# Router step of the second half moved ahead of the first half's final layer norm, and five weight tensors stored partition-major

## The reference

```python
x = x + _layernorm(_L0_attn_ref(_layernorm(x), ...))
x = x + _layernorm(_L0_ffn_ref(_layernorm(x), ...))

# attention: conv of width 3 (4096 -> 3072), q/k/v projections 1024 -> 1024,
# causal attention inside blocks of 128 tokens, 16 heads of 64,
# output projection wo (1024 -> 1024), then proj_w (1024 -> 4096)

# ffn
logits = einsum('bsh,he->bse', hidden_states, gate_w)        # 8 experts
routing_weights, _ = top_k(logits, 2)
h = relu(hidden_states @ up_w) ** 2                          # 4096 -> 8192
shared_out = h @ down_w                                      # 8192 -> 4096
x_latent = hidden_states @ fc1_w                             # 4096 -> 2048
expert_out = x_latent @ expert_w                             # 2048 -> 2048
moe_out = expert_out * sum(routing_weights)                  # one number per token
routed_out = moe_out @ fc2_w                                 # 2048 -> 4096
return _layernorm(shared_out + routed_out)
```

## Time and profile before

| | |
|---|---|
| median of 3 runs | 4912.88 us (4912.10 to 4917.04) |
| the profiled execution | 4912.69 us |
| its span on the slowest core (core 4) | 4911.6 us |
| spans of the 8 cores | 4874.0 to 4911.6 us |
| TensorE busy | 3857.2 us, 79% of the span |
| VectorE, ScalarE, GpSimd busy | 761.7, 488.3, 273.3 us |
| granted TensorE clock, mean of a core | 0.906 to 0.910 of full speed |

### The profile page before, as it was taken

The page is one execution under the profiler, slowest core; times in us unless marked ns, Lnnn a source line. Parts: engine busy times, 40 slices in busy tenths (PEclk is TensorE's granted clock), DMA queues, the critical chain, the costliest instruction groups (busy, mean ns, idle before and its releaser), DMA issues.

```text
span 4911.6 us, 43172 instructions; the slowest of 8 cores (4874.0 to 4911.6 us)
## 1 busy us (share of the span) xinstructions
PE 3857.2 (79%) x18033; PEld 1726.2 (35%) x18033; DVE 761.7 (16%) x1126; ACT 488.3 (10%) x797; POOL 273.3 (6%) x369
## 2 busy tenths in 40 slices
PE   1699999999548711889998999970779998999960
PEld 1244444444223201334443444430334443444420
DVE  4300000000460144110000000027110000000027
ACT  2100000002213411001111000002001111000001
POOL 0000000000000022000000000000000000000000
PEclk9999999999769855899999999995899999999985
DMA  5144444446002243668887776763578887677743
GB/s 160 35 75 75 76 75 75 75 77 103 0 1 44 62 161 150 122 115 153 152 152 139 135 144 130 143 127 123 112 123 150 156 153 136 132 140 143 141 89 113
DMA packets 80495, 548.40 MB, mean 112 GB/s; under 512 B 7146, under 2 KB 15786, under 8 KB 34219
## 3 DMA queue, kind: packets, MB, share of 16 engines
q0 software_dynamic: 68304, 444.68, 51.2%
q1 hardware_dynamic: 12000, 100.96, 5.8%
HBM read 948.33 MB, written 41.94 MB: 202 GB/s over the span
## 4 chain that ended last, share of the span: by engine, by line
PE 74%; DVE 11%; DMA 10%; issue 2%; POOL 1%; SPq 1%; ACT 1%; DVEq 0%; ACTq 0%; POOLq 0%
PE ps L957 21%; PE ps L442 20%; PE ps L1112 18%; DVE pool L179 11%; PE ps L1050 5%; DMA pool<-fc1w 2%; PE ps L705 2%; DMA pool<-x 2%; PE ps L1012 1%; POOL pool L775 1%; DMA pool<-x2sp 1%; PE ps L708 1%; PE ps L511 1%; DMA pool<-expw 1%; DMA pool<-fc2w 1%
## 5 line engine op out<-in xcount | busy, mean ns | idle before, releaser
L957 PE MATMUL ps<-pool 128*128 128x512 bf16 x5120 | 1120.9, 382 | 55.3 <-DMA pool<-fc1w 33.3
L442 PE MATMUL ps<-pool 128*128 128x512 bf16 x4608 | 998.8, 379 | 0.9 <-DVE pool L179 0.9
L1112 PE MATMUL ps<-pool 128*128 128x512 bf16 x4096 | 898.7, 380 | 46.9 <-DMA pool<-fc2w 46.6
L957 PEld LDWEIGHTS ps<-pool 128*128 128x128 bf16 x5120 | 501.4, 98 | 676.9 <-issue 86.3
L442 PEld LDWEIGHTS ps<-pool 128*128 128x128 bf16 x4608 | 445.6, 97 | 553.8 <-issue 4.4
L179 DVE CAST pool<-ps 128x512 bf16<-128x512 f32 (+1 forms) x192 | 107.1, 558 | 3340.6 <-PE ps L1050 1997.9
L1112 PEld LDWEIGHTS ps<-pool 128*128 128x128 bf16 x4096 | 397.4, 98 | 526.2 <-issue 54.5
L179 ACT ACTIVATE pool<-pool 128x512 bf16<-128x512 f32 (+4 forms) x251 | 231.8, 923 | 1951.2 <-DVE pool L179 1778.1
L179 ACT ACTIVATE pool<-ps 128x512 f32<-128x512 f32 (+1 forms) x256 | 152.8, 597 | 1351.7 <-PE ps L957 1240.6
L1050 PE MATMUL ps<-pool 128*128 128x512 bf16 x1024 | 231.5, 379 | 0.0
L179 DVE TENSOR_TENSOR pool<-pool 128x1 f32<-128x1 f32 (+3 forms) x226 | 173.5, 768 | 263.6 <-ACT pool L179 189.2
(11 more groups left out here) (63 smaller groups left out, 983.7 us busy)
## 6 DMA issues: line engine op xcount, KB each, us to landing
pool<-upw POOLq DMA_DIRECT2D x128, 1024.0 KB, 8.8
pool<-downw POOLq DMA_DIRECT2D x64, 2048.0 KB, 14.3
pool<-wconv POOLq DMA_DIRECT2D x72, 1024.0 KB, 16.7
pool<-x SPq DMA_DIRECT2D x16, 2048.0 KB, 9.5
pool<-fc1w POOLq DMA_DIRECT2D x32, 1024.0 KB, 8.5
pool<-fc2w POOLq DMA_DIRECT2D x32, 1024.0 KB, 19.7
x2sp<-pool SPq DMA_DIRECT2D x8, 2048.0 KB, 6.3
pool<-expw POOLq DMA_DIRECT2D x16, 1024.0 KB, 9.2
```

What stands on the lines that cost most here:

```text
L442: it = te.matmul(pbf[bk], sl[:, k * 128 : (k + 1) * 128], t1T[:, k * 1026 + base : k * 1026 + base + 512], start=(dw == 0 and k == 0), sto ...
L957: it = te.matmul(pbf[bk], slots[s][:, k * 128 : (k + 1) * 128], rhs_fn(k), start=(k == 0), stop=(k == n_k - 1))
L1112: te.matmul(pbf[bk], dw_sl[s][:, k * 128 : (k + 1) * 128], hup[:, k * 512 : (k + 1) * 512], start=(k == 0), stop=False)
```

## The change

There are two independent edits.

**Edit 1, order.** The router step becomes a function `gate_top2(half)`, with the same instructions. For half 0 it is called where it stood. For half 1 it is called directly behind `load_t2(1)`, ahead of half 0's final layer norm. Nothing of its instructions, banks or buffers differs; the last value of `rwb` is kept for each half in a dictionary.

**Edit 2, layout.** wq, wk, wv, wo and the eight proj slices are stored in DRAM with the partition as the outer axis. A load of wq, wk, wv or wo reads one run of 32 KB for each partition instead of 8 runs of 4 KB; a proj slice reads one run of 16 KB instead of 8 of 2 KB. The bytes in SBUF are the same. The rearrangement is done on the host, ahead of the launch.

```diff
-    dproj = nc.dram_tensor("projw", [8, WDC, 128, 512], F32, kind="ExternalInput").ap()
+    dproj = nc.dram_tensor("projw", [8, 128, WDC, 512], F32, kind="ExternalInput").ap()
...
-    p.inc(po.dma_start(wq_sb.rearrange("p (k c) -> p k c", k=WDC), dwq.rearrange("k p c -> p k c")), "WQ", 16)
+    p.inc(po.dma_start(wq_sb.rearrange("p (k c) -> p k c", k=WDC), dwq), "WQ", 16)
...
         ins = po.dma_start(proj_sl[s].rearrange("p (k c) -> p k c", k=WDC),
-                           dproj[og].rearrange("k p c -> p k c"))
+                           dproj[og])
...
-    load_t2(0)
-    p.wait(te, "SC")
-    tb_free[0] = tb_free[1] = p.cnt["SV"]
-    for half in range(2):
-        if half == 1:
-            p.wait(po, "SP", down_done)
-            if dtaps:
-                p.wait(po, "SA")
-                p.wait(sy, "SA")
-
+    rwb_ready_h = {}
+
+    def gate_top2(half):
         p.wait(te, "SA", t2_loads[half])
         p.wait(te, "WQ", cg)
         last_rw_t = 0
...
         bank_free[3] = ("SV", rwb_ready)
+        rwb_ready_h[half] = rwb_ready
+
+    load_t2(0)
+    p.wait(te, "SC")
+    tb_free[0] = tb_free[1] = p.cnt["SV"]
+    for half in range(2):
+        if half == 1:
+            p.wait(po, "SP", down_done)
...
+        else:
+            gate_top2(0)
+        rwb_ready = rwb_ready_h[half]
...
         if half == 0:
             p.wait(sy, "SP", down_done)
             load_t2(1)
+            gate_top2(1)
 
         p.wait(ve, "SV", s_ready)
```

More of the change, by code:

```diff
@@ L196, in build @@
     dwconv = nc.dram_tensor("wconv", [W3C, 3, 128, DC, 128], F32, kind="ExternalInput").ap()
[L197 to L200, removed]
-    dproj = nc.dram_tensor("projw", [8, WDC, 128, 512], F32, kind="ExternalInput").ap()
+    dwq = nc.dram_tensor("wq", [128, WDC, 1024], F32, kind="ExternalInput").ap()
+    dwk = nc.dram_tensor("wk", [128, WDC, 1024], F32, kind="ExternalInput").ap()
+    dwv = nc.dram_tensor("wv", [128, WDC, 1024], F32, kind="ExternalInput").ap()
+    dwo = nc.dram_tensor("wo", [128, PAIRS, 1024], F32, kind="ExternalInput").ap()
+    dproj = nc.dram_tensor("projw", [8, 128, WDC, 512], F32, kind="ExternalInput").ap()
     dprojbr = nc.dram_tensor("projb_row", [1, D], F32, kind="ExternalInput").ap()
@@ L454, in build @@
     c_ready = p.cnt["SC"]
-    p.inc(po.dma_start(wq_sb.rearrange("p (k c) -> p k c", k=WDC), dwq.rearrange("k p c -> p k c")), "WQ", 16)
-    p.inc(po.dma_start(wk_sb.rearrange("p (k c) -> p k c", k=WDC), dwk.rearrange("k p c -> p k c")), "WK", 16)
+    p.inc(po.dma_start(wq_sb.rearrange("p (k c) -> p k c", k=WDC), dwq), "WQ", 16)
+    p.inc(po.dma_start(wk_sb.rearrange("p (k c) -> p k c", k=WDC), dwk), "WK", 16)
     if "c" in dtaps:
@@ L484, in build @@
     p.wait(po, "SP")
-    p.inc(po.dma_start(wv_sb.rearrange("p (k c) -> p k c", k=WDC), dwv.rearrange("k p c -> p k c")), "WV", 16)
-    p.inc(po.dma_start(wo_sb.rearrange("p (k c) -> p k c", k=PAIRS), dwo.rearrange("k p c -> p k c")), "WO", 16)
+    p.inc(po.dma_start(wv_sb.rearrange("p (k c) -> p k c", k=WDC), dwv), "WV", 16)
+    p.inc(po.dma_start(wo_sb.rearrange("p (k c) -> p k c", k=PAIRS), dwo), "WO", 16)
     fb = {0: bank_free[0], 1: bank_free[1]}
@@ L933, in build @@
         bank_free[3] = ("SV", rwb_ready)
+        rwb_ready_h[half] = rwb_ready
[5 more added lines that the diff above has]
+            p.wait(po, "SP", down_done)
+            if dtaps:
+                p.wait(po, "SA")
+                p.wait(sy, "SA")
+        else:
+            gate_top2(0)
+        rwb_ready = rwb_ready_h[half]
         def p1(n_m, n_k, dram_fn, rhs_fn, evac_fn, slots, slot_init, dsem):
@@ L1181, in prep_weights @@
     for nm, key in (("wq", "L0_attn_wq"), ("wk", "L0_attn_wk"), ("wv", "L0_attn_wv")):
-        w[nm] = np.ascontiguousarray(np.asarray(inp[key]).reshape(WDC, 128, 1024))
-    w["wo"] = np.ascontiguousarray(np.asarray(inp["L0_attn_wo"]).reshape(PAIRS, 128, 1024))
+        w[nm] = np.ascontiguousarray(
+            np.asarray(inp[key]).reshape(WDC, 128, 1024).transpose(1, 0, 2))
+    w["wo"] = np.ascontiguousarray(
+        np.asarray(inp["L0_attn_wo"]).reshape(PAIRS, 128, 1024).transpose(1, 0, 2))
     w["projw"] = np.ascontiguousarray(
-        np.asarray(inp["L0_attn_proj_w"]).reshape(WDC, 128, 8, 512).transpose(2, 0, 1, 3))
+        np.asarray(inp["L0_attn_proj_w"]).reshape(WDC, 128, 8, 512).transpose(2, 1, 0, 3))
     w["projb_row"] = np.ascontiguousarray(np.asarray(inp["L0_attn_proj_b"]).reshape(1, D))
```

## The result

| | before | changed |
|---|---|---|
| the profiled execution | 4912.69 us | 4920.74 us |
| its span on the slowest core | 4911.6 us (core 4) | 4919.7 us (core 7) |
| median of 30 runs each, all runs | 4922.07 us | 4928.97 us |
| median of the runs below 5000 us | 4914.9 us (17 runs) | 4924.2 us (22 runs) |
| ratio of the undisturbed runs | | 1.0025, 95% interval 1.0013 to 1.0036 |

The changed kernel is 0.25% slower, some 12 us. The medians over all runs differ by 6.9 us only, because 13 of the 30 runs before and 8 of the 30 changed ones took over 5000 us, up to 640 us longer than the others (in the changed ones a die shows a lower granted clock), and I go by the ratio, which leaves these out.

The account below looks back on a forecast made before the run. TensorE bounds 74% of the chain; the half seam, where VectorE's layer norm holds the chain, decides. Order +13.8 us, layout -1.2, together +12.7 on 4912.7, hence 4925.5 us, 0.26% slower; range 4918 to 4931 for 8 in 10.

Parts of the forecast that it names:

- the base of the sum: Starting time for the forecast: the profiled 4912.7 us, moved 0.2 us to the median of the runs shown, 4912.88.
- The t2 load comes out from under the layer norm: Half seam: load time unchanged at 30.7 us but no longer covered; VectorE starts the layer norm 44.3 us later.
- the rival of a faster load: SP's four t2 loads speed up with nothing beside them; at its end 25.9 us saved, 4899.5 us; chance 0.04.
- the row sum: Sign at half 0's final layer norm: VectorE's first row sum near 3340.6, less 1 or 2 for the layout change.
- Layer norm shorter by the first x2 wait: Half 0's final layer norm: first x2 piece already there, so 151.1 us instead of 156.3, the 5.25 us wait gone.
- Blocks 0 and 1 under the layer norm: TensorE runs two fc1 blocks during the layer norm, then stops; router, block 0 and a load, 32.6 us, leave the path.
- The rival in which it doesn't: fc1's blocks 0 and 1 follow the layer norm instead of running under it; 4936 us; chance 0.04.
- The bare store: After the layer norm: fc1's first CAST waits for the last output store, now uncovered, 4.8 us from issue to landing.
- The ramp: fc1 after the long TensorE idle restarts at half clock and loses 1.6 us, bounds 0 and 3.2.
- Edit 2: Layout change: wait for the first proj slice falls 11.62 to 10.45, 1.2 us saved; projection weight loads give nothing.
- Nothing later gives it back: From fc1's block 4 on, both kernels alternate a load and two blocks alike, so the order change's +13.8 us stays.
- block 4's load: Measuring point in half 1's fc1: issued when block 2 is done, forecast to shift by 13.8 us.

Follow-up runs that it names:

- edit 2 alone: The kernel before with only the weight layout changed, router order kept; ratio to the kernel before 0.9990, 95% interval 0.9978 to 1.0003.
- edit 1 alone: The kernel before with only the router order changed, all weights in their old layout; ratio to the kernel before 1.0032.
- router after tile 0: The changed kernel with half 1's router called between the first and second tile of half 0's final layer norm; ratio to the kernel before 0.9965.
- fc1's output moved: The changed kernel with fc1's output buffer and the expert weight slots exchanged in SBUF; ratio to the kernel before 1.0014.
- woven kernel: The changed kernel with router after the layer norm's first tile, fc1 output and expert slots exchanged, 12 fc1 copies inside later tiles; ratio to before 0.9836.

## Why the prediction was right, and where it was not

**The step that failed is the base of the sum.** The prediction put its +12.7 us on 4912.7 and moved it by 0.2 to the median of the three runs shown. Over 30 runs the median before is 4922.07, 9.2 us above that base; over the runs below 5000 us it is 4914.9, 2.0 above it. So the forecast of 4925.5 lies only 3.4 us above the kernel before as measured over all runs, where the medians differ by 6.9. That 4928.97 still lies within 4918 to 4931 is luck: the same +12.7 on 4922.07 gives 4934.7. Three runs within 5 us of each other did not show where the median of 30 would lie: 7.1 us above that of the runs below 5000 us for the kernel before, and 4.7 for the changed one. The change itself was sized right, +0.26% for 0.25% by the ratio, and its terms follow.

- **The t2 load comes out from under the layer norm: right.** Its time didn't change (29.1 to 31.0 us, before 29.4 to 30.7), so the rival of a faster load falls, and the row sum moved by 43.5 us for 44.3.
- **Layer norm shorter by the first x2 wait: right in kind, too large.** From the first row sum to the last store it took 151.4 us for 154.9 before, 3.6 less by unrounded times where 5.1 was forecast; the other x2 waits grew a little on some cores (up to 8.2 us at a time, at most 7.4 before). This and the 0.8 us of the term above partly cancel: the last store moved by 40.0 for 39.2.
- **Blocks 0 and 1 under the layer norm: right.** TensorE got ahead exactly as far as two banks allow. The rival in which it doesn't is out.
- **The bare store: right**, 4.0 to 4.6 us from issue to the CAST for 4.8. Taking it away gave the time back.
- **The ramp: right in kind.** Blocks 2 and 3 took 15.3 to 16.6 us together on the eight cores, where two blocks at full clock take 14.0: 1.3 to 2.6 us, for 1.6. The two windows of core 7 show the granted clock, 0.51 while TensorE idles and 0.85 over block 2:

```profile
3357.00:3495.00 138.00, 0.00 (x0) 0.00 (x0) 99.01 (x54) 28.80 (x28) 0.53 (x1) 0.51 0.36 123
3496.00:3505.00 9.00, 8.94 (x36) 3.83 (x37) 0.98 (x2) 0.00 (x0) 0.02 (x1) 0.85 0.01 2
```

- **Edit 2: right.** -1.2 us was forecast, -1.4 in the mean wait of edit 2 alone and -1.2 in the changed kernel. The projection weights' loads were hidden.
- **"Nothing later gives it back": right.** The median of the expert start moved by 11.9 us only, but the stretch from block 4's load to the expert start did not get shorter: 104.8 to 113.7 us before, mean 109.0, and 104.3 to 112.7, mean 108.9, in the changed kernel. By the means block 4's load moved by 13.7 us and the expert start by 13.6. The same stretch has a mean of 106.7 us with edit 1 alone and 105.9 with edit 2 alone, so some 3 us of scatter between executions remain.

## What to carry to other kernels

Moving a small step forward on an in-order engine also moves every wait it contains in front of what stood there: ask what the step's first wait was covered by, and put it behind just enough of the old work to keep that cover (here one tile of four turned +0.25% into -0.35%). The large idle time next to it, 129 us before and 140 after, came from VectorE's order: fc1's copies had to be woven into the layer norm before TensorE could use it. Together with the router after tile 0, which alone gave 0.35%, and fc1's output moved, that was worth 1.6%. And when a wait is moved to another queue, as the stores' wait was to the expert loads, look for it again as soon as something else gets faster. And a difference of 0.2% can be forecast well and still be lost in the base: three runs were too few to say where the median of 30 lies.

## What the runs showed of the hardware

- A 1 MB weight load with 16 KB instead of 2 KB of source per run took 0.53 instead of 0.87 us to issue, and landed in a median of 7.8 to 7.9 us on six of eight cores (edit 2 alone; 9.3 and 9.8 on the other two) and of 7.8 to 8.0 on all eight (changed), against 8.6 to 10.4 before. Both run lengths are above the 512 bytes that the Trainium skill (DMA: Bandwidth & Descriptors, section "Specifications") gives as enough for line rate. The trace does not agree that nothing is left to gain above it, for loads from GpSimd that cast. The number of runs fell with their length, from 1024 to 128, and which of the two it was is not shown.
- After 138 us of work TensorE's clock stayed full over an idle of 2.0 to 2.7 us, and the next block ran at full clock (granted clock 1.00 over its first 4 us on core 1). After 3.0 to 4.1 us it fell to half, at once on core 3 (0.50 over the first 2 us), within the first 2 us on core 0 (0.81, then 0.50). The idle alone doesn't decide: in the changed kernel, on core 5, an idle of 2.63 us after 14.0 us of work was followed by two blocks that took 15.66 us, with a granted clock of 0.71 over the first 2 us and then 0.50.
- An x2 load of 1 MB from SP landed in 6.9 us alone and in a median of 13.5 us, up to 17.5, beside fc1's 1 MB loads from GpSimd (woven kernel, core 0). VectorE's longest wait for one grew from 6.1 us before to 15.9 on this core.
